# Graph attention with residual and layer norm: an ending of its own for the last two pairs, on every engine

## The reference

```python
q, k, v = heads(x @ Wq + bq), heads(x @ Wk + bk), heads(x @ Wv + bv)
scores = einsum("bhqd,bhkd->bhqk", q, k) / sqrt(64)
probs = softmax(scores + where(adj, 0, -9e15), axis=-1)
ctx = einsum("bhqk,bhkd->bhqd", probs, v)          # heads side by side again
y = x + ctx @ Wf + bf
out = (y - mean(y)) / sqrt(var(y) + 1e-5)          # over the 384 features
```

## Time and profile before

| | |
|---|---|
| median of 3 runs | 1042.59 us (1041.44 to 1043.32) |
| the profiled execution's own time | 1043.51 us |
| its span, first to last instruction | 1041.7 us |
| busy: TensorE matmuls | 1018.4 us (98%) |
| busy: VectorE | 734.5 us (71%) |
| busy: GpSimd | 631.9 us (61%) |
| busy: ScalarE | 593.6 us (57%) |
| DMA, mean | 172 GB/s |

### The profile page before, as it was taken

One profiled execution on the slowest core, in us unless ns is written; L12 is line 12 of the kernel. 1 busy time (PEld: TensorE's weight loads), 2 busy tenths in 40 slices (PEclk: granted clock), 3 DMA queues, 4 the chain that ended last, 5 costly groups with the idle time before them and its releaser, 6 DMA issues.

```text
span 1041.7 us, 26751 instructions
## 1 busy us (share of the span) xinstructions
PE 1018.4 (98%) x7161; PEld 906.6 (87%) x7161; DVE 734.5 (71%) x2823; ACT 593.6 (57%) x2119; POOL 631.9 (61%) x652
## 2 busy tenths in 40 slices
PE   8999999999999999999999999999999999999975
PEld 7889889888888889889889889888888888888865
DVE  3576777777777677677677677677777777777564
ACT  3565655655655655656656656656656656656550
POOL 1356666666666666666656666665665665665675
PEclk9999999999999999999999999999999999999998
DMA  7276666676676676676676676676676676664443
GB/s 194 68 207 179 180 178 174 181 190 164 179 189 164 178 192 163 177 193 160 178 190 166 180 189 165 180 190 164 183 185 165 184 186 166 185 182 147 145 137 122
DMA packets 338971, 179.63 MB, mean 172 GB/s; under 512 B 222593, under 2 KB 322561, under 8 KB 338945
## 3 DMA queue, kind: packets, MB, share of 16 engines
q1 hardware_dynamic: 338544, 178.74, 63.7%
q10 hardware_dynamic: 400, 0.59, 0.2%
HBM read 103.75 MB, written 75.50 MB: 172 GB/s over the span
## 4 chain that ended last, share of the span: by engine, by line
PE 95%; DVE 2%; DMA 1%; POOL 1%; issue 1%; SPq 0%; DVEq 0%; POOLq 0%
PE qk_ps L339 14%; PE cov_ps L339 13%; PE cov_ps L341 13%; PE cov_ps L340 13%; PE qk_ps L341 13%; PE qk_ps L340 13%; PE scores_ps L355 9%; PE cov_ps L369 8%; DMA s_mask<-in_L_gnn_Wk 1%; DMA probs<-in_L_gnn_Wv 1%; DVE s_mask L501 0%; DVE stats L539 0%; DVE y_sb L533 0%; SPq L251 0%; DVE wv_lo L469 0%
## 5 line engine op out<-in xcount | busy, mean ns | idle before, releaser
L629 ACT ACTIVATE probs<-s_mask,neg_max 128x128 f32<-128x128 f32 x768 | 297.4, 391 | 6.9 <-DVE neg_max L507 6.9
L501 DVE CUSTOM_DVE_ANT_0 s_mask<-scores_ps,mask_bias 128x128 f32<-128x128 f32 x768 | 172.6, 287 | 95.2 <-PE scores_ps L355 91.1
L720 POOL TENSOR_TENSOR probs<-probs,inv_sum 128x768 f32<-128x768 f32 x128 | 189.1, 1478 | 80.0 <-DVE inv_sum L520 80.0
L715 POOL TENSOR_SCALAR y_sb<-y_sb,mean_var,rstd 128x384 f32<-128x384 f32 x127 | 210.1, 1655 | 23.4 <-POOL rstd L709 23.4
L513 DVE STREAM_TRANSPOSE p_turned<-probs 128x768 f32<-128x768 f32 x128 | 125.2, 978 | 116.2 <-POOL probs L720 116.2
L709 POOL TENSOR_TENSOR rstd<-var_eps,minus_half 128x1 f32<-128x1 f32 x128 | 72.3, 565 | 178.9 <-DVE var_eps L545 178.9
L647 ACT ACTIVATE qT<-qk_ps,bq_col 128x512 f32<-128x512 f32 x96 | 65.6, 684 | 154.1 <-PE qk_ps L341 154.1
L629 ACT ACTIVATION_READ_ACCUMULATOR probs<-s_mask,neg_max 128x1 f32 x768 | 145.5, 189 | 0.0
L339 PE MATMUL cov_ps<-wf_hi,cT_hi 128*128 128x384 f32 x384 | 130.7, 340 | 11.5 <-DVE cT_lo L475 11.5
L622 ACT CAST cT_hi<-cov_ps 128x384 fp32r<-128x384 f32 x128 | 61.5, 480 | 137.5 <-PE cov_ps L369 134.7
L490 DVE TENSOR_TENSOR xT_lo<-xT,xT_hi 128x384 fp32r<-128x384 f32 x120 | 113.0, 980 | 32.9 <-ACT xT_hi L616 32.7
(11 more groups left out here) (57 smaller groups left out, 1974.0 us busy)
## 6 DMA issues: line engine op xcount, KB each, us to landing
p_out<-p_turned SPq DMA_DIRECT2D x128, 384.0 KB, 2.6
pT<-p_out SPq DMA_DIRECT2D x512, 96.0 KB, 2.4
x_in<-in_x SPq DMA_DIRECT2D x128, 192.0 KB, 3.5
out<-y_sb SPq DMA_DIRECT2D x128, 192.0 KB, 2.4
x_blocks<-in_x SPq DMA_DIRECT2D x360, 64.0 KB, 2.4
adj_u<-in_adj SPq DMA_DIRECT2D x32, 64.0 KB, 3.2
y_sb<-in_L_gnn_Wq ACTq DMA_DIRECT2D x1, 576.0 KB, 4.6
s_mask<-in_L_gnn_Wk SPq DMA_DIRECT2D x1, 576.0 KB, 6.5
```

Of the source, the lines that this page charges most:

```text
L501: last = nc.vector.tensor_tensor_reduce(out=s_mask[:, e, h, :], in0=scores_ps[:, score_cols(e, h)], in1=mask_bias[:, e, :], scale=SCALE, s ...
L629: last = nc.scalar.activation(probs[:, e, h, :], s_mask[:, e, h, :], ACT.Exp, bias=neg_max[:, e, h:h + 1], scale=1.0, accum_out=row_sum[:, ...
L715: nc.gpsimd.tensor_scalar(y_sb[:, y, :], y_sb[:, y, :], mean_var[:, e, 0:1], rstd[:, e, 0:1], ALU.subtract, ALU.mult).then_inc(y_ready, 1)
L720: nc.gpsimd.tensor_tensor(probs[:, e, :, :], probs[:, e, :, :], inv_sum[:, e, :].unsqueeze(2).broadcast_to([P, HEADS, SEQ]), ALU.mult).the ...
```

## The change

Steps 0 to 61 run as before, except that V of pairs 62 and 63 is no longer computed in steps 60 and 61 (`ENDING` = 62). In place of steps 62 to 65 every engine has a function `ending` with an order written out by itself:

- TensorE: scores 62, context 60, output 60, scores 63, context 61, V 62, output 61, V 63, context 62, output 62, context 63, output 63. Late V goes into the `qk_ps` banks; V of pair 63 waits for the copy of V of pair 62 from the same bank.
- VectorE: residual adds and statistics of pair 60 and the mask of element 126 come ahead of the transpose of element 124, and so on, as in the diff. It normalises the last four elements (`BY_VECTOR` = 124) instead of the last one.
- ScalarE: the V copies of pair 62 follow each element's exponentials of pair 63.
- GpSimd: both pairs' mask biases and x plus bias are done earlier; the normalisation of 120 comes between the probabilities of 125 and 126, that of 121 behind the probabilities of 127. For elements 124 to 127 it computes the power alone.
- SyncE: the loads of an element follow its store directly; y of pair 60 is stored between the store and the loads of element 127, y of pairs 61 to 63 behind them.

Waits that were written with `past` are in several places written with `wait_ge` for the same value.

```diff
+ENDING = PAIRS - 2
+BY_VECTOR = BATCH - 4
@@ SyncE
+            def ending():
+                a, b = ENDING, ENDING + 1
+                load_blocks(a // TURN, a % TURN - 1, 1, 2 * (a - 1) + 1)
+                for e in range(2):
+                    store_y(a - 3, e)
+                for q in (a, b):
+                    i, c = q // TURN, q % TURN
+                    store_blocks(c, 0, 2 * q)
+                    load_blocks(i, c, 0, 2 * q)
+                    store_blocks(c, 1, 2 * q + 1)
+                    if q == b:
+                        for e in range(2):
+                            store_y(a - 2, e)
+                    load_blocks(i, c, 1, 2 * q + 1)
+                for q in (a - 1, a, b):
+                    for e in range(2):
+                        store_y(q, e)
@@ TensorE
-                if isinstance(p, int) and p - 1 + AHEAD >= PAIRS:
+                if isinstance(p, int) and p - 1 + AHEAD >= ENDING:
                     past(pe, y_added, n - 2)
+                    past(pe, v_copied, n)
...
+            def late_v(q, e):
+
+                past(pe, xT_split, 2 * q + e)
+                pe.wait_ge(qk_copied, GROUPS * NJ)
+                if q > ENDING:
+                    past(pe, v_copied, 2 * (q - 1) + e)
+                v_product(qk_ps[e], 2 * q + e)
...
-                if real(p + AHEAD, PAIRS):
-                    for e in range(2):
-                        v_product(c, p, e)
+                if real(p + AHEAD, ENDING):
+                    for e in range(2):
+                        early_v(c, p, e)
+
+            def ending():
+                a, b = ENDING, ENDING + 1
+                for q in (a, b):
+                    for e in range(2):
+                        scores(q // TURN, q % TURN, e, 2 * q + e)
+                    for e in range(2):
+                        ctx_product(q // TURN, q % TURN, q, e)
+                    if q == b:
+                        for e in range(2):
+                            late_v(a, e)
+                    for e in range(2):
+                        out_product(q % TURN, q, e)
+                for e in range(2):
+                    late_v(b, e)
+                for p in (a + LAG, b + LAG):
+                    for e in range(2):
+                        ctx_product(p // TURN, p % TURN, p, e)
+                    for e in range(2):
+                        out_product(p % TURN, p, e)
@@ VectorE
+            def normalise_last(p, e):
+                n = 2 * p + e
+                dve.wait_ge(rstd_ready, n + 1)
+                nc.vector.tensor_scalar(y_sb[:, n % Y_RING, :], y_sb[:, n % Y_RING, :], mean_var[:, e, 0:1],
+                                        rstd[:, e, 0:1], ALU.subtract, ALU.mult).then_inc(last_y_ready, 1)
...
+                for e in range(2):
+                    mask_and_max(e, 2 * a + e)
+                for e in range(2):
+                    split_ctx(e, 2 * (a - 2) + e)
+                add_residual(*at(a), 0, 2 * (a - 2))
+                invert_sums(0, 2 * a)
+                add_residual(*at(a), 1, 2 * (a - 2) + 1)
+                find_stats(a % TURN, 0, 2 * (a - 2))
+                mask_and_max(0, 2 * b)
+                turn_blocks(*at(a), 0, 2 * a)
+                invert_sums(1, 2 * a + 1)
+                for e in range(2):
+                    split_ctx(e, 2 * (a - 1) + e)
+                turn_blocks(*at(a), 1, 2 * a + 1)
+                mask_and_max(1, 2 * b + 1)
+                invert_sums(0, 2 * b)
+                find_stats(a % TURN, 1, 2 * (a - 2) + 1)
+                add_residual(*at(b), 0, 2 * (a - 1))
+                turn_blocks(*at(b), 0, 2 * b)
+                invert_sums(1, 2 * b + 1)
+                add_residual(*at(b), 1, 2 * (a - 1) + 1)
+                find_stats(b % TURN, 0, 2 * (a - 1))
+                turn_blocks(*at(b), 1, 2 * b + 1)
+                find_stats(b % TURN, 1, 2 * (a - 1) + 1)
+                for q in (a, b):
+                    p = q + LAG
+                    for e in range(2):
+                        split_ctx(e, 2 * q + e)
+                    if q == b:
+                        for e in range(2):
+                            normalise_last(a, e)
+                    for e in range(2):
+                        add_residual(*at(p), e, 2 * q + e)
+                        find_stats(p % TURN, e, 2 * q + e)
+                for e in range(2):
+                    normalise_last(b, e)
@@ ScalarE
+                for e in range(2):
+                    round_ctx(e, 2 * (a - 2) + e)
+                for e in range(2):
+                    exps(e, 2 * a + e)
+                for e in range(2):
+                    round_ctx(e, 2 * (a - 1) + e)
+                for e in range(2):
+                    exps(e, 2 * b + e)
+                    copy_v(qk_ps[e], (2 * a + e) % V_RING, 2 * a + e)
+                for e in range(2):
+                    copy_v(qk_ps[e], (2 * b + e) % V_RING, 2 * b + e)
+                for q in (a, b):
+                    for e in range(2):
+                        round_ctx(e, 2 * q + e)
@@ GpSimd
+                for e in range(2):
+                    make_mask_bias(a // TURN, a % TURN, e, 2 * b + e)
+                for e in range(2):
+                    add_bias(a // TURN, a % TURN, e, 2 * a + e)
+                normalise_probs(0, 2 * a)
+                for e in range(2):
+                    add_bias(b // TURN, b % TURN, e, 2 * b + e)
+                normalise_probs(1, 2 * a + 1)
+                normalise_y(a % TURN, 0, 2 * (a - 2))
+                for e in range(2):
+                    normalise_probs(e, 2 * b + e)
+                normalise_y(a % TURN, 1, 2 * (a - 2) + 1)
+                for q in (a - 1, a, b):
+                    for e in range(2):
+                        normalise_y((q + LAG) % TURN, e, 2 * q + e)
```

More of the change, by code:

```diff
@@ L284, in load_blocks, with store_y @@
                                  ).then_inc(pT_landed[slot], DMA)
+            def store_y(p, e):
+                n = 2 * p + e
+                if n >= BY_VECTOR:
+                    sp.wait_ge(last_y_ready, n - BY_VECTOR + 1)
+                else:
+                    past(sp, y_ready, n)
+                sp.dma_start(out[n, :, :], y_sb[:, n % Y_RING, :]).then_inc(y_stored[n % Y_RING], DMA)
             def step(i, c):
@@ L314, in step @@
                         slot = (2 * (c - STORE_LAG) + e) % Y_RING
-                        if isinstance(n, int) and n == BATCH - 1:
-                            sp.wait_ge(last_y_ready, 1)
-                        else:
-                            past(sp, y_ready, n)
+                        past(sp, y_ready, n)
                         sp.dma_start(out[bass.ds(n, 1), :, :].rearrange("b p d -> p (b d)"), y_sb[:, slot, :]
@@ L327, in step @@
                     store_blocks(c, 1, 2 * p + 1)
-            run_steps(sp, step, PAIRS + STORE_LAG, PAIRS // TURN - 2)
+            def ending():
[15 more added lines that the diff above has]
+                        store_y(q, e)
+            run_steps(sp, step, ENDING, PAIRS // TURN - 2)
+            ending()
             for slot in range(Y_RING):
@@ L453, in step @@
                     qk_product(i, c, j)
[L454 removed]
+                if real(p + AHEAD, ENDING):
                     for e in range(2):
[L456 removed]
+                        early_v(c, p, e)
[18 more added lines that the diff above has]
+                        out_product(p % TURN, p, e)
             pe.wait_ge(ident_ready, 2)
             warm_up(WARM_UPS[-1])
[L460 removed]
+            run_steps(pe, step, ENDING)
+            ending()
         @block.vector
@@ L540, in find_stats @@
                 past(dve, y_stats, n)
-                past(dve, y_ready, n - 2)
+                if isinstance(n, int) and n - 2 >= BY_VECTOR:
+                    dve.wait_ge(last_y_ready, n - 1 - BY_VECTOR)
+                else:
+                    past(dve, y_ready, n - 2)
                 apart(dve)
@@ L591, in step, with ending, at @@
                     find_stats(c, 1, 2 * (p - LAG) + 1)
-            run_steps(dve, step, PAIRS + LAG)
+            def ending():
+                a, b = ENDING, ENDING + 1
+                def at(q):
+                    return q // TURN, q % TURN
+                for e in range(2):
[34 more added lines that the diff above has]
+                    normalise_last(b, e)
+            run_steps(dve, step, ENDING)
+            ending()
         @block.scalar
@@ L669, in step, with ending @@
                     copy_qk(i, c, j)
-                if real(p + AHEAD, PAIRS):
+                if real(p + AHEAD, ENDING):
                     for e in range(2):
-                        copy_v(c, e, 2 * (p + AHEAD) + e)
-            run_steps(act, step, PAIRS + LAG)
+                        copy_v(cov_ps[e], (2 * (c + AHEAD) + e) % V_RING, 2 * (p + AHEAD) + e)
+            def ending():
+                a, b = ENDING, ENDING + 1
+                for e in range(2):
[12 more added lines that the diff above has]
```

(10 more changed lines are left out.)

47 lines of the change are left out of this document (22 added, 25 removed).

## The result

| | before | after |
|---|---|---|
| median, 5 runs each | 1042.59 us | 1037.02 us |
| ratio, 95% interval | | 0.9941 (0.9930 to 0.9953) |
| profiled execution's own time | 1043.51 us | 1037.02 us |
| its span | 1041.7 us | 1035.2 us |

The change makes the kernel 5.57 us faster, where 8.2 had been forecast: right in sign and inside the range, 2.6 us short. It is a small gain, 0.6% by the ratio, but the interval lies clear of 1. On two other chips the same kernel took 1037.39 (beside 1043.29 for the kernel before) and 1036.54 (beside 1042.46).

The account below looks back on a forecast made before the run. TensorE was taken to bound the kernel until the ending, then SyncE's queue sets the pace. Gains 2.12 + 3.41 + 3.84 = 9.37, less 1.2 for the clock, gave 8.2 us: 1034.4, range 1031.5 to 1038.5.

Parts of the forecast that it names:

- rival 3: SyncE's queue in the ending: one or two steps are dear, 1.7 and 0.9 us; 1036.1 to 1037.0; chance 0.14.
- Part 1: Steps 60 and 61: without V of pairs 62 and 63, scores of pair 62 start 5.48 us earlier.
- Rival 4: Steps 60 and 61: something other than TensorE holds the old pace; gain only 2.7 us, 1039.9; chance 0.04.
- Part 2: VectorE's new order in step 62 gives back 3.36 of the 5.48 us; store of 124 is 2.12 earlier.
- Part 3: SyncE's store and load chain for the last four elements sets the pace: 19.41 instead of 22.82 us, gain 3.41.
- y's stores and the adds of pair 62: Ending: VectorE's adds wait for y's stores to land; second add ends near 1021, hidden by 2 us.
- Part 4: Late V in TensorE's gaps of the ending: all 36 matmuls hide, with 1.6 us to spare.
- Part 5: From the last load's landing to the last normalisation: 6.43 instead of 10.27 us, gain 3.84.
- Part 6: TensorE's granted clock: a low stretch over the last output products costs 1.2 us, bounds 0 and 2.5.
- Rival 1: No low clock stretch over the last products: gain 9.4 us, 1033.2; chance 0.25.
- rival 2: Clock falls after every gap, also before pair 60's output product, about 1.5 us more: gain 6.7, 1035.9; chance 0.11.

Follow-up runs that it names:

- e4_early_v: Changed kernel with V of pairs 62 and 63 computed in steps 60 and 61 again, late V left out; 1041.45 us, ratio 0.9983.
- e2_turn_first: Changed kernel with VectorE's transpose of element 124 moved between the adds of 120 and 121, inversion ahead, mask of 126 behind the statistics; 1033.45 us, ratio 0.9902.
- e6_nops48: Changed kernel with 48 empty TensorE instructions ahead of the output product of pair 60; 1037.12 us, ratio 0.9944.
- e0_after_again: The changed kernel run again without edit on a second chip; 1037.39 us.
- e5_act_queue: e2_turn_first with the store and loads of element 127 issued by ScalarE's DMA queue instead of SyncE's; 1031.90 us, ratio 0.9897.
- e8: e5_act_queue with 4 and 8 small unused transposes ahead of the two context products of pair 63; 1031.68 us, ratio 0.9897.
- e10: e2_turn_first with 4 and 8 unused transposes (alone 1032.66 us) plus 48 empty instructions ahead of pair 60's output product; 1032.37 us, ratio 0.9908.
- e7_warm: Changed kernel with 16 and 8 small unused transposes ahead of the context products of 126 and 127; 1035.61 us, ratio 0.9934.
- e3_gpsimd_norm: Changed kernel with elements 124, 125 and 126 normalised by GpSimd again, only 127 by VectorE; 1037.51 us, ratio 0.9951.

## Why the prediction was right, and where it was off

The range held, because it had been drawn out as far as rival 3 with slow products. The number that came, 1037.02, is not near the forecast of 1034.4 (chance 0.42) but at the upper edge of rival 3's 1036.1 to 1037.0 (chance 0.14), and rival 3 is also what happened in the main: one of SyncE's steps was dear, by 2.2 us. The interval behind the landing, 0.75 longer than priced, made up the rest. What follows takes the parts one by one.

**Part 1, V's place:** right. Scores of 62 at 990.50, forecast 991.35 less 0.88, that is 990.47; TensorE waited 0.78 for the q copy that V had covered. e4_early_v shows 5.3 us for the move, forecast 5.48. Rival 4 (another engine holds steps 60 and 61) falls with it.

**Part 2, VectorE's order:** right to the hundredth, 12.31 from the scores to the store of 124. e2_turn_first takes exactly the 3.36 us back (8.95) and the time follows by 3.9. So the new order of VectorE in step 62 had been a cost, and it could be taken back.

**Part 3, SyncE's queue:** right as the mechanism, and here lies the step that failed. The sum priced the store of 126 at 2.66 to its loads, by the two rows nearest to it; it took 4.88 in the first trace, 4.40 and 4.17 in the others. That is 2.2 of the missing 2.6 us (the other links came in 0.3 below their prices, so the interval was 21.3 instead of 19.4). The prediction had read the row that tells it, a longest wait of 3.9, and set it down as rival 3, at a chance of 0.14. It had not asked where that wait lay and what lay beside it. The waits of SyncE's queue for `p_out`, in after, first from 200 to 950 us and then from 960 to 1036:

```profile
SPq L284 <- DMA p_out<-p_turned: 39.2, 37, 2.0
```

```profile
SPq L284 <- DMA p_out<-p_turned: 22.8, 10, 4.4
```

In the 47 steps of the loop that the first window holds, no such wait is longer than 2.0 us; in the ending two are 4 and more. These waits tell less than they seem to, for in the loop SyncE issues other transfers between a store and its loads, and that time is no wait. The transfers of the blocks themselves, from issue to landing, reach 3.4 us in the same window (4.0 in before), so company other than q8 costs something too:

```profile
DMA to landing us min/median/max: 1.9/2.5/3.4
```

The DMA view of the same kernel has no q8 packet at all from 200 to 950. In the ending there are three of 16 KB from 955 us on, at 979.5, 993.7 and 1011.7, and each dear piece stands on one. The q8 row, of after at 979 to 980 and 1011 to 1012, of before at 979 to 980 and 1020 to 1021, of e6_nops48 at 1010 to 1011, of e2_turn_first at 1011 to 1012 (packets, MB, share):

```profile
q8 instruction: 1, 0.02, 5.9%
...
q8 instruction: 1, 0.02, 12.6%
```

```profile
q8 instruction: 1, 0.02, 6.1%
...
q8 instruction: 1, 0.02, 6.0%
```

```profile
q8 instruction: 1, 0.02, 5.8%
```

```profile
q8 instruction: 1, 0.02, 5.5%
```

In both kernels the packet at 979 to 980 meets the store of element 121 (977.66 in after, whose loads start at 982.26). The one of before at 1020 meets the four loads that took 2.67. That of after at 1011 meets the store of 126 at 1011.32; in e6 and e2 it meets loads, which take 2.58 and 2.46, and the store keeps to 2.6. The packet at 993.7 of after meets the loads of 123, which take 2.55.

The packet records of all 14 traces, from 955 us on, say the same without exception. Of 34 hops that hold a packet, the 19 in which it starts up to 2.0 us behind the store take 3.84 to 4.97 us; the 15 in which it starts 2.3 us or more behind, near the hop's end, take 2.60 to 3.04; the 90 without a packet take 2.31 to 3.00. Sets of four loads take 1.72 to 1.76 us in the 115 cases without a packet, and 1.73 to 3.24 in the 23 with one. And there is one place where only some traces have a packet, near 964 us, at the two loads of `x_in`: after and before have none, the other twelve have one. SyncE there, in after and in e0_after_again, whose packet starts at 964.3:

```profile
963.88 0.89 SPq L254 DMA_DIRECT2D x_in<-in_x  x2
```

```profile
964.41 1.71 SPq L254 DMA_DIRECT2D x_in<-in_x  x2
```

It takes 0.89 us in the two without and 1.39 to 1.81 in the twelve with. So a q8 packet early in a hop goes with 1.2 to 2.4 us more for it, and mostly 0.1 to 1.1 more for a set of loads, in e4_early_v 1.5. No run took the packet away, and its place was moved on purpose only once, and little (e6); but SyncE's chain and the packets were shifted against each other in e2, e4, e5 and e8 to e10 as well, and the dear piece was each time the one that the packet met. That each dear piece goes with a packet is shown. How it makes the others late is not: it takes 0.9 to 2.0 us itself (12.6% of 16 engines in one us are 2.0), and hops with a packet of 0.9 us are as dear as with one of 2.0.

**y's stores and the adds of pair 62:** hidden, as forecast, but with 0.2 us to spare and not 2. VectorE in after:

```profile
1021.33 0.56 DVE L595 TENSOR_TENSOR y_sb<-cov_ps,x_bias 128x384 f32<-128x384 f32 x1 [4.05 <-DMA out<-y_sb]
...
1023.30 0.56 DVE L595 TENSOR_TENSOR y_sb<-cov_ps,x_bias 128x384 f32<-128x384 f32 x1 [0.31 <-issue]
...
1024.87 0.55 DVE L537 TENSOR_TENSOR cT_lo<-cov_ps,cT_hi 128x384 fp32r<-128x384 f32 x1
```

It waited 4.05 us for the store of y of 120. The add of 125, for which the context product of 127 also waits, ended at 1023.86, where the prediction had it near 1021 (1020.1 on this axis), and that product came at 1024.11. The store landed 2.9 us behind its issue at 1018.44, where 2.2 had been taken, and the issue was late by the dear store of 126. In the faster e5_act_queue this wait has caught up with the loads.

**Part 4, V in the gaps:** right. Late V ended at 1011.5 and the context product behind it still waited 2.85 us for the loads of 125.

**Part 5, behind the landing:** right in kind, 0.75 us too small. Without a low clock the interval is 7.0 to 7.2 (e4, e7 to e10), forecast 6.43. The prediction let the output products start at once, since the split of 126 had been done by then. It had not: VectorE was still in the adds and statistics of pair 62, which had waited for y's stores, and began that split at 1024.87 (above), 0.76 behind the landing. So in e7_warm 1.21 us pass from context product to output product instead of 0.78, and from the add of 127 to the last normalisation 2.5 instead of 2.2. VectorE's normalisation is worth 0.6 of the gain (e3_gpsimd_norm). The larger part is that TensorE waits for VectorE 1.21 us behind the landing and not 2.26, and that the statistics of 127 follow its add by 0.59 us and not, behind those of 126, by 1.44.

**Part 6, the clock:** right. A low stretch lay over the last products in every trace of after, it cost 1.1 us (by the traces of after and e7_warm), forecast 1.2, and 2.4 in e6. Rival 1 falls, rival 2 too: the 1.7 us gap ahead of the output product of pair 60 did not lower the clock: in after the products behind it follow 0.17 apart, as before it.

The sum by its own terms, then: forecast 8.2; 2.2 for the store of 126, less 0.3 for the other links, 0.75 for the interval behind the landing, 0.1 back for the clock: 5.65 us, where 5.57 were measured. That it closes to 0.1 us is partly luck: the terms are those of one trace, and the hop of 126 alone was 4.88, 4.40 and 4.17 in the three traces of after.

## What to carry to other kernels

When an ending is a chain through one DMA queue, write the chain down link by link and look for the instruction that starts it: moving the first transpose of the chain ahead of one add, one set of statistics and one mask in VectorE's order gave 3.4 us, more than the normalisations, the second queue and the clock together. In pricing such a chain, look up the longest wait of its kind, where it lies, and what the other queues did there, before it is called an accident. Test in the trace whether the stretch being priced has company that the steady part of the kernel has not.

## What was not expected

- A single 16 KB packet of the instruction queue q8, early in a hop, goes with 1.2 to 2.4 us more for the 384 KB store of that hop, and with up to 1.5 us more in the issue of four loads: 19 hops of 19, and 22 of 23 sets of loads above the 1.76 us that none without a packet passes.
- Empty instructions ahead of a loop (80 of them) left the packets behind the loop where they were and cost nothing in the median (1037.37 beside 1037.39); 48 in a gap of 1.74 us did not delay the product behind it.
- 24 transposes without use, in 3.7 us of idle time of TensorE, kept the granted clock at 1.00 and shortened the last interval by 1.1 us.
- A second DMA queue let the last store start 2.4 us earlier and the product behind its loads only 0.3 us: the transfers had slowed, and an add of VectorE that waits for y's stores ended 0.1 us before that product.
